# A transformer block on one core: POOL takes more of the quantised feed-forward, ACT's gelu and DVE's next inner row change places with rounding and largest, and the projection's rows are normalised further ahead

## What is computed

```python
x = x + L0_xattn(layernorm(x), ctx)          # 8 heads, 77 keys
x = x + L0_ffn(layernorm(x))                 # below
x = x + L1_xattn(ctx, layernorm(x), mask)    # 4 heads of 64, keys from ctx and x, RMS-normalised
x = x + L1_ffn(layernorm(x))                 # routed experts, top 2 of 8, and a shared one

def bitlinear(x, W, b):                      # per-tensor ternary W, 8-bit rows
    w_scale = clip(mean(|W|), 1e-5); Wq = clip(round(W / w_scale), -1, 1) * w_scale
    x_scale = clip(max(|x|, axis=-1), 1e-5)
    xq = clip(round(x * 127 / x_scale), -128, 127) * x_scale / 127
    return xq @ Wq.T + b
def L0_ffn(x):                               # 256 -> 1024 -> 256
    return bitlinear(gelu(bitlinear(x, W1, b1)), W2, b2)
```

## Time and profile before

| | |
|---|---|
| median of 3 runs | 929.47 us (927.81 to 930.09) |
| the profiled execution | 928.22 us |
| its span, first to last instruction | 926.5 us |
| mean granted clock of PE | 0.987 of full speed |
| feed-forward | about 53 to 142 us of the span |
| projection to the start of attention | about 127 to 200 us |

### The profile page before, as it was taken

How to read it: one execution, slowest core, us unless ns; L and a number is a source line. 1 busy time by engine, 2 the same in 40 slices (tenths; PEclk the granted TensorE clock), 3 DMA queues, 4 the chain that set the end, 5 groups by cost and what they waited for, 6 DMA issues and landing times.

```text
span 926.5 us, 14997 instructions
## 1 busy us (share of the span) xinstructions
PE 866.8 (94%) x4299; PEld 611.3 (66%) x4300; DVE 630.7 (68%) x1275; ACT 532.6 (57%) x851; POOL 388.9 (42%) x334
## 2 busy tenths in 40 slices
PE   9977789889999999999999999999999999999992
PEld 4635455545555555555457887878888888888881
DVE  5788987855567557456488779846666666666666
ACT  2558885445665765775554534326666666666650
POOL 2144455435676746756515545512222222222210
PEclk9999999989999999999999999999999999999997
DMA  9400000009478578569565100078711298526405
GB/s 310 110 1 1 0 1 1 1 5 364 160 292 328 194 305 326 219 269 350 199 262 196 82 1 1 12 316 342 305 40 36 71 348 341 208 88 254 116 9 182
DMA packets 49909, 154.07 MB, mean 166 GB/s; under 512 B 6266, under 2 KB 24438, under 8 KB 44236
## 3 DMA queue, kind: packets, MB, share of 16 engines
q1 hardware_dynamic: 46124, 144.25, 41.4%
q0 software_dynamic: 3744, 9.31, 3.1%
HBM read 97.85 MB, written 56.62 MB: 167 GB/s over the span
## 4 chain that ended last, share of the span: by engine, by line
PE 67%; DVE 17%; ACT 6%; issue 3%; DMA 3%; POOL 2%; SPq 1%; DVEq 0%; ACTq 0%; POOLq 0%
PE banks L1047 11%; PE banks L1300 8%; PE banks L1302 8%; PE banks L1301 8%; PE banks L1015 4%; PE banks L1039 3%; PE banks L1040 3%; DVE small L2105 2%; PE banks L1337 2%; PE banks L1339 2%; PE banks L1338 2%; PE banks L1313 2%; PE banks L953 2%; PE banks L919 1%; PE banks L1061 1%
## 5 line engine op out<-in xcount | busy, mean ns | idle before, releaser
L1047 PE MATMUL banks<-wexp 128*65 128x512 f32 (+1 forms) x288 | 149.9, 602 | 3.5 <-ACT wexp L1614 3.5
L677 POOL TENSOR_TENSOR cv_hl<-wexp,cv_hl 128x1024 fp32r<-128x1024 f32 x45 | 108.6, 2421 | 56.0 <-ACT cv_hl L1591 55.4
L1300 PE MATMUL banks<-ring,x_hi 128*128 x312 | 127.5, 408 | 0.0
L1302 PE MATMUL banks<-ring,x_lo 128*128 x312 | 122.1, 391 | 0.0
L1301 PE MATMUL banks<-ring,x_hi 128*128 x312 | 122.0, 391 | 0.0
L1614 ACT ACTIVATE wexp<-banks 128x512 f32<-128x512 f32 x128 | 76.4, 599 | 64.2 <-PE banks L1040 63.8
L2105 DVE TENSOR_REDUCE small<-banks 128x1 bf16<-128x1107 f32 x64 | 84.1, 1314 | 38.4 <-PE banks L1015 38.4
L1750 ACT ACTIVATE banks<-wexp 128x1024 f32 x72 | 73.5, 1021 | 47.7 <-DVE aux L2496 47.7
L1728 ACT ACTIVATE aux<-banks 128x512 f32<-128x512 f32 x78 | 46.7, 599 | 61.2 <-PE banks L1302 45.2
L1039 PE MATMUL banks<-q_hi,k_hl 128*128 128x512 f32 x144 | 76.7, 533 | 1.9 <-ACT q_lo L1582 1.0
L1302 PEld LDWEIGHTS banks<-ring,x_lo 128*128 128x128 f32 x312 | 58.6, 188 | 13.2
(11 more groups left out here) (374 smaller groups left out, 2171.5 us busy)
## 6 DMA issues: line engine op xcount, KB each, us to landing
wsplit<-cv_hl SPq DMA_DIRECT2D x45, 1024.0 KB, 8.0
ring<-wsplit SPq DMA_DIRECT2D x32, 1280.0 KB
wexp<-in_L_ffn_w SPq DMA_DIRECT2D x40, 512.0 KB, 5.9
wexp<-in_expert_biases SPq DMA_DIRECT2D x8, 1152.0 KB, 6.6
ring<-wsplit SPq DMA_DIRECT2D x4, 1024.0 KB, 8.2
wexp<-moe_y SPq DMA_DIRECT2D x7, 512.0 KB, 6.1
wexp<-in_L_ffn_sw SPq DMA_DIRECT2D x5, 512.0 KB, 9.0
x_sb<-in_x SPq DMA_DIRECT2D x4, 512.0 KB, 7.6
```

Of the source, the lines that this page charges most:

```text
L677: g.tensor_tensor(sides(hl[:, PIECE:2 * PIECE]), raw, sides(hl[:, 0:PIECE]).bitcast(f32), ALU.subtract).then_inc(s['cv_lo'], 1)
L1047: mm(pb[5 + half][0:DA, :], vh[b][0:w, c, :], pT[q % 3][0:w, :], start=c == 0, stop=c == len(KTILES) - 1).then_inc(s['a_pv'], 1)
L1300: mm(o[:], x_hi[u][:, kc, :], hi, start=kc == 0 and not primed, stop=False, skip_group_check=primed)
L1302: last = mm(o[:], x_lo[u][:, kc, :], hi, start=False, stop=primed and kc == KC - 1, skip_group_check=primed)
```

## The change

It moves work between engines and changes the order in two queues.

- DVE's `ffn_sum` is gone. ACT scales the second layer's result out of PSUM into one of two new buffers `y_part`, and POOL adds it to `x_sb` six tiles behind its normalising. DVE's statistics follow one turn later and wait for POOL (`f_res`).
- POOL rounds the tokens in place of ACT, except for the last tile. Its normalising is written as x * rstd + less_mean, where DVE prepares less_mean = -mean * rstd. The constants of attention, which it set after the feed-forward, are set between the tiles.
- ACT's gelu of tile i+2 comes before the rounding of tile i+1.
- DVE's row of tile i+2 comes before the two largest of the turn.
- PE turns tile i+4's tokens in turn i, between the second layer of tile i and the transposes of tile i+1.
- In the projection, tiles 6 and 7 are normalised and the scales of tiles 8 to 15 are made before any squares are summed; after that tile t+6 is normalised in step t, where it was t+4.
- Two semaphores for constants are merged into one, which does not change the order of anything, and the matmuls that fill a pause in turn -3 write another bank.

```diff
@@ POOL
+            def ffn_tokens(t):
+                g.tensor_scalar(xn[:, t % 2, :], xn[:, t % 2, :], f_by[:, t % 2, 0:1], MAGIC, ALU.mult, ALU.add).then_inc(s['f_xm'], 1)
+            def ffn_result(t):
+                pool.wait_ge(s['f_yout'], t + 1)
+                g.tensor_tensor(x_sb[:, t, :], x_sb[:, t, :], y_part[t % 2], ALU.add).then_inc(s['f_res'], 1)
             for t in range(T):
                 if t == TB:
                     pool.wait_ge(s['f_rstd'], 2)
                 if t >= 2:
                     pool.wait_ge(s['f_xqT_full'], t - 1)
-                g.tensor_scalar(xn[:, t % 2, :], x_sb[:, t, :], mv[:, t, 0:1], rstd[:, t:t + 1], ALU.subtract, ALU.mult).then_inc(s['f_xn'], 1)
+                g.tensor_scalar(xn[:, t % 2, :], x_sb[:, t, :], rstd[:, t:t + 1], less_mean[:, t:t + 1], ALU.mult, ALU.add).then_inc(s['f_xn'], 1)
+                if t >= 1:
+                    pool.wait_ge(s['f_by'], t)
+                    ffn_tokens(t - 1)
                 pool.wait_ge(s['f_xn'], t + 1)
-                if t >= 5:
-                    pool.wait_ge(s['f_by'], t)
                 g.tensor_tensor(x_sb[:, t, :], x_sb[:, t, :], b2_all[:], ALU.add).then_inc(s['f_pool'], 1)
+                if t >= 6:
+                    ffn_result(t - 6)
+                if 8 <= t < 13:
+                    pool.wait_ge(s['f_res'], t - 5)
+                    attention_constants(t - 8)
...
+            for t in range(T - 6, T):
+                ffn_result(t)
@@ PE, ffn_turn
                 if there(i + 3):
                     ffn_in(i + 3, 1 - u)
                 if there(i):
                     ffn_out(i, u)
+                if there(i + 4):
+                    ffn_tokens_T(i + 4, u)
                 if there(i + 1):
                     ffn_hidden_T(i + 1, 1 - u)
@@ ACT
-                if there(tokens):
+                if isinstance(tokens, int) and tokens == T - 1:
                     a(xn[:, u, :], xn[:, u, :], ACT.Copy, scale=f_by[:, u, 0:1], bias=MAGIC).then_inc(s['f_xm'], 1)
...
+            def ffn_sum(t, u):
+                act.wait_ge(s['f_y'], t + 1)
+                act.wait_ge(s['f_by'], t + 5)
+                if not isinstance(t, int) or t >= 2:
+                    act.wait_ge(s['f_res'], t - 1)
+                a(y_part[u], pb[6][:, 0:D], ACT.Copy, scale=f_step[:, 1 - u, 1:2]).then_inc(s['f_yout'], 1)
             def ffn_turn(i, u):
-                if there(i + 3):
-                    ffn_T(i + 3, 1 - u)
+                if there(i - 1):
+                    ffn_sum(i - 1, 1 - u)
                 if there(i):
                     ffn_hidden_T(i, u)
+                if there(i + 2):
+                    ffn_act(i + 2, u)
                 if there(i + 4) or there(i + 1):
                     ffn_quantise(i + 4, i + 1, i, u)
-                if there(i + 2):
-                    ffn_act(i + 2, u)
+                if there(i + 4):
+                    ffn_T(i + 4, u)
@@ DVE
             def ffn_scales(t0, t1):
                 norm(t0, t1, 0.0)
-                ve.sem_inc(s['f_rstd'], 1)
+                v.scalar_tensor_tensor(less_mean[:, t0:t1], mv[:, t0:t1, 0], -1.0, rstd[:, t0:t1], ALU.mult, ALU.mult).then_inc(s['f_rstd'], 1)
...
             def ffn_turn(i, u):
-                if there(i - 1):
-                    ffn_sum(i - 1, 1 - u)
                 if there(i + 1):
                     ve.wait_ge(s['f_acc'], i + 2)
...
-                if there(i - 1):
-                    ffn_statistics(i - 1)
+                if there(i + 2):
+                    ffn_hidden(i + 2, u)
                 if there(i + 4):
                     last = ffn_tokens(i + 4, u)
                 if there(i + 1):
                     last = ffn_largest(i + 1, 1 - u)
...
                     ffn_factors(u, c)
-                if there(i + 2):
-                    ffn_hidden(i + 2, u)
+                if there(i - 2):
+                    last = ffn_statistics(i - 2)
@@ DVE, projection
+            for t in range(6, TB):
+                proj_tokens(t)
+            scales(LN_EARLY, T, ln_r, 1.0 + LN_EPS, LN_EPS ** 2)
             for t in range(T):
...
-                if 6 <= t + 4 < T:
-                    proj_tokens(t + 4)
+                if TB <= t + 6 < T:
+                    proj_tokens(t + 6)
                 proj_squares(t)
-                if t == 3:
-                    scales(LN_EARLY, T, ln_r, 1.0 + LN_EPS, LN_EPS ** 2)
```

More of the change, by code:

```diff
@@ L192, in program @@
         h_qT = [scr.take(HID, HC, bf16) for _ in range(2)]
+        y_part = [scr.take(D) for _ in range(2)]
         assert scr.at <= mark
@@ L272, in program @@
         ln_r = sb("ln_r", [P, T])
+        less_mean = sb("less_mean", [P, T])
         gateT = sb("gateT", [P, KC, E])
@@ L784, in full, with warm @@
                 last.then_inc(s['prep_full'], 1)
-            def warm(n):
+            def warm(n, o=pb[7]):
                 for _ in range(n):
-                    mm(pb[7][:], ones_b[:], ones_b[:].unsqueeze(1).to_broadcast([P, 4, P]), start=True, stop=True)
-            pe.wait_ge(s['warm'], 1)
+                    mm(o[:], ones_b[:], ones_b[:].unsqueeze(1).to_broadcast([P, 4, P]), start=True, stop=True)
+            pe.wait_ge(s['const'], 2)
             warm(28)
-            pe.wait_ge(s['const'], 2)
+            pe.wait_ge(s['const'], 3)
             pe.wait_ge(s['ld_l0'], NLD['ld_l0'])
@@ L898, in _, with ffn_tokens_T @@
             pe.wait_ge(s['f_pre'], 2)
-            def ffn_in(t, u):
+            def ffn_tokens_T(t, u):
                 pe.wait_ge(s['f_xm'], t + 1)
@@ L904, in ffn_in @@
                 last.then_inc(s['f_xqT_full'], 1)
+            def ffn_in(t, u):
                 pe.wait_ge(s['f_xqT'], t + 1)
@@ L964, in between @@
                 if i == -3:
-                    warm(WARM_FFN)
+                    warm(WARM_FFN, pb[5])
                 if i == T - 4:
@@ L1983, in ffn_hidden @@
                 v.scalar_tensor_tensor(h_f[u], banks[:, 2 * (1 - u) * 512:2 * (2 - u) * 512], f_step[:, u, 0:1], b1_all[:], ALU.mult, ALU.add).then_inc(s['f_acc'], 1)
-            def ffn_sum(t, u):
-                ve.wait_ge(s['f_y'], t + 1)
-                ve.wait_ge(s['f_pool'], t + 1)
-                v.scalar_tensor_tensor(tile(t), pb[6][:, 0:D], f_step[:, 1 - u, 1:2], tile(t), ALU.mult, ALU.add)\
-                    .then_inc(s['f_yout'], 1)
             def ffn_statistics(t):
-                ve.wait_ge(s['f_yout'], t + 1)
-                statistics(t)
+                ve.wait_ge(s['f_res'], t + 1)
+                return statistics(t)
             def ffn_turn(i, u):
-                if there(i - 1):
-                    ffn_sum(i - 1, 1 - u)
                 if there(i + 1):
@@ L2002, in ffn_turn @@
                     c = slice(0 if there(i + 3) else 1, 2 if there(i) else 1)
+                    if not isinstance(i, int) or i >= 2:
+                        ve.wait_ge(s['f_yout'], i - 1)
                     last = v.tensor_tensor(f_step[:, 1 - u, c], f_max[1 - u][:, c], wsc[:, c], ALU.mult)
-                    if not there(i + 1):
+                    if isinstance(i, int) and i < 0:
                         link(last)
-                if there(i - 1):
-                    ffn_statistics(i - 1)
+                    elif not there(i + 1):
+                        last.then_inc(s['f_by'], 1)
+                        ve.wait_ge(s['f_by'], i + 5)
+                if there(i + 2):
+                    ffn_hidden(i + 2, u)
                 if there(i + 4):
@@ L2015, in ffn_turn @@
                     ffn_factors(u, c)
-                if there(i + 2):
-                    ffn_hidden(i + 2, u)
+                if there(i - 2):
+                    last = ffn_statistics(i - 2)
+                    if isinstance(i, int) and i == T - 7:
+                        link(last)
             ss_l = p0[:].rearrange("p a b -> p (a b)")
```

23 lines of the change are left out of this document (16 added, 7 removed).

## The result

The change makes the kernel slower: a median of 958.95 us against 929.06 (927.81 to 930.09) on the same chip, ratio 1.0315 (1.0291 to 1.0339). One of its four executions was slow (1183.65 us) and is left out of the ratio; the other three took 955.89 to 959.03 us (median 958.88). That is +29.9 us where +24.1 was forecast, and inside the range. The profiled execution took 959.03 us.

The account below looks back on a forecast made before the run. PE, busy for 94% of the span, was taken as the kernel's bound, DVE as the feed-forward's. To the end of tile 13's transposes 22.7, then 1.0, projection 0.4: +24.1 us on 929.47, say 953.5, range 944.5 to 961.

Parts of the forecast that it names:

- The loop through the two buffers: Feed-forward: DVE's early row waits for transposes that free its buffer, closing a one-turn loop of 5.56 us, before 4.40.
- POOL's rounding at 1.22 us, a turn of 6.0: Feed-forward: POOL's token rounding takes 1.22 us and delays PE's eight transposes, adding 0.45 to a turn: 6.0 us.
- The clock, a rival with 0.20: Feed-forward loop: PE's clock falls in half the turns, transposes take about 0.7 us more, 4.6 in all: 958; chance 0.20.
- quick rounding: Rival, feed-forward: POOL rounds quickly, 12 x 0.45 less in the turns and 0.4 on the way in: 948; chance 0.23.
- The way in, +0.7: Up to row 2 of the feed-forward: POOL's rounding, less_mean and a later gelu table cost +0.7 us (0 to 1.5).
- The end of the feed-forward: Tile 13's transposes end at 150.2 us, +22.7; on to projection tile 3, gelu before tile 14's rounding adds +1.0.
- ACT's order, no price of its own in the turn: Feed-forward: with gelu ahead of rounding and the other swaps, ACT's turn stays near 3.7 us.
- The projection, +0.4: From projection tile 3 on: later squares on POOL against some savings, net +0.4 us, between -2 and +3.3.
- a sign that the prediction had set for itself as one of being wrong: Projection: the distance from tile 3 to head 0's transposes changing by over 3 us would make the prediction wrong.
- my upper bound of 3.3: Projection: POOL's backlog of squares arrives in full at head 0's transposes, +3.3 us.
- The 2 us that I took off for engines standing ready: Projection: ACT will stand ready, with no projection rows queued ahead of the root, so 2 us of the backlog is hidden.
- the 0.9 at the end: Projection: three normalisings gone from DVE's queue behind the mean squares give some 0.9 us back.

Follow-up runs that it names:

- before_multiply_add: The kernel before, with POOL's normalising written as a multiplication and an addition in place of a subtraction and a multiplication: 925.17 us, ratio 0.9953.
- fill_pe: The kernel after, with eight matmuls of 256 columns, whose result nothing reads, added in PE's pause in each turn: 952.11 us, ratio 1.0265.
- dve_order_back: The kernel after, with DVE's row of tile i+2 alone back at the end of its turn: 939.98 us, ratio 1.0125.
- proj_order_alone: The kernel before, with only the projection's order of the kernel after: 926.03 us, ratio 0.9968.
- pool_split_new_loop: The kernel after, with POOL squaring projection tiles 0 and 1 between its last results and DVE summing those squares before the scales: 955.29 us, ratio 1.0292.
- before_row_first: The kernel before, with DVE writing the row of tile i+2 ahead of the two largest: 951.95 us, ratio 1.025.
- dve_act_order_back: The kernel after, with DVE's row and ACT's gelu back in their old places: 929.23 us, ratio 1.0002.

## Why the prediction was right, and where it was not

*The loop through the two buffers.* Shown in both directions: the order alone makes it in the kernel before (+23 us), the order undone or a third buffer takes it away. It was right step by step and not only in its sum: in the turn shown no step is more than 0.06 us from the working. Its warm length, 5.50 to 5.58, is the 5.56 of the working.

*POOL's rounding at 1.22 us, a turn of 6.0.* Wrong: 0.47, and the turn of 5.56 held. The term was mis-sized because L616, the nearest row, owes its length to its form (subtract and multiply), which `before_multiply_add` shows. Twelve turns at 6.0 gave 72.0 us; they took 68.94.

*The clock, a rival with 0.20.* That the clock falls is in the earlier trace rows; the 0.7 us that a cold turn was to take more, and the half of the turns that were to be cold, were estimates that no run shows: it was 0.47 to 0.90, in three turns of twelve. The fall came beside quick rounding, though with shorter turns than I had joined it to. The cold turns cost 0.90 + 0.47 + 0.57 = 1.9 us over 5.55 from row 2 to 14; row 1 to row 2 is 6.42 (0.9; granted clock 0.50 from 73.59 to 75.11); tile 13's transposes 1.86 (0.8; 0.54 while they run); tile 0 of the projection 4.36 for 2.75 (1.6; 0.50 from 152 to 154). That is 5.2 up to projection tile 3; `fill_pe`, warm in all of them, is 4.6 shorter from row 0 (61.79) to tile 3 (160.75) than after. I had 4.6 for this rival. Rounding that was quicker than forecast (12 x 0.45 = 5.4 less) and a colder clock (5.2 more) about cancel. Two terms were wrong by some 5 us each, in opposite directions, so the closeness of the total is luck.

*The way in, +0.7.* Wrong, +2.8. Row 2 is the first to need a used buffer, so row 1 to row 2 is already a turn of the loop: 4.19 before, 5.58 in `fill_pe` (68.01 to 73.59), 6.42 cold. I counted the loop from row 2 on and should have counted 13 turns.

*The end of the feed-forward.* 22.7 and +1.0 forecast, 22.5 and 2.0 measured. That 22.5 meets 22.7 is luck: quick rounding took 5.4 off, the cold clock put 3.6 on up to there, and the thirteenth turn, which I had not counted, 1.4 (5.58 for 4.19). The excess of the second is the cold tile 0.

*ACT's order, no price of its own in the turn.* The turn shown bears that out, since the longer loop hides it. It is not free in general: with DVE's row back in its place it costs some 10 us (`dve_order_back`).

*The projection, +0.4.* The step that failed most: +5.0 to the first score. From tile 3 to head 0's transposes it is 28.44 us for 25.21, 3.2 more, and over 3 was a sign that the prediction had set for itself as one of being wrong; so was a granted clock other than the 1.00 that it forecast for the feed-forward (0.92 from row 2 to row 14). The reason given held: squares of tile 2 at 9.5 us after tile 3 (forecast 9), mean squares at 20.5 (21), head 0's transposes 3.2 later, my upper bound of 3.3. In the 9.5 some luck is hidden: the scales started at 3.7 for 3, their chain took 4.7 for 6, and the last 1.1, mostly DVE's sum of tile 0's squares, was not in my 9. The 2 us that I took off for engines standing ready and the 0.9 at the end were not there. From mean squares to head 0's transposes it is 7.96 us, before 7.48.

But against `proj_order_alone` (6.3 from tile 3 to the squares of tile 2) it is not the order that costs. After has 3.1 us more there: 1.1 because tile 15's statistics wait for the result's new way through ACT and POOL (tile 3 + 1.8 for + 0.7), 0.7 for two rows normalised beside POOL's squares (1.46 for 0.73), and 1.3 for the chain of scales beside them. Another 0.9 lies between mean squares and head 0 (7.96 for 7.08, of which L2101 itself is 0.8, held beside POOL), and 2.3 behind it, where PE is cold behind a pause of 4.71 us (1.97 and 4.25 us for 1.09 and 2.75; granted clock 0.50 from 194.65 to 196.62). With the order's own gain, -1.4, this makes 4.9 of the 5.0. So the loss belongs to the part that I had down as a gain without a price, POOL's larger share: its results stand in front of its squares, and some of DVE's small instructions (L1905, L2101) end only with its own. The split of POOL's queue gives some 3 us of medians back, within touching intervals.

*The sum.* In medians +29.9 for +24.1: of the 6.7 that the span is over the sum, the turns are -3.0, the way in 2.1, the two stretches behind the loop 1.7, the projection and what follows 5.9.

Open is why three turns of twelve go cold when PE's pauses in front of all are alike (before L924 1.57, 1.57 and 1.71 us in the cold turns, up to 1.72 in warm ones). In `pool_split_new_loop`, the same loop, it is other turns: those that end at 87.04, 104.58 and 122.11 (6.27, 6.45 and 6.45 us), where in after they end at 92.64, 115.25 and 132.51. Open too is what PE's own new order is worth: its queue is the third that the change reorders, and no run undoes that. In the turn shown it costs nothing, as the two token transposes are through (102.35) before ACT's rounding ends (102.47).

## What to carry to other kernels

With two buffers, an instruction that refills one may stand no earlier in its queue than the work that frees the other: lay out the way from refill to release, and count every engine's queue on it, and every turn from the first reuse. A part that frees the busiest engine is worth its work only if what it queues on the other engine is in front of nothing that is due; here the work moved to POOL, with the orders back, gained up to 4 us in the loop and lost them at the next stage, until two pieces were taken out of the line. Where a loop leaves PE pauses like those here (1.57 and 1.71 us in front of the cold turns of after, 2.20 in the turn shown of `before_row_first`), look at the granted clock before costing its transposes, and behind the loop too (4.71 us in front of head 0).

## What the runs showed of the hardware

- POOL's tensor_scalar on 128 x 256 takes 1224 ns as subtract and multiply with two scalars from memory, 555 as multiply and add with two (`before_multiply_add`), and 475 as multiply and add with one scalar and a constant (L614, after).
- Some of DVE's instructions, small as they are, ended when POOL's did: L1905 on 8 columns 1.03 us (170.53 to 171.56) beside POOL's L676 (170.49 to 171.53), the mean squares L2101 1.00 beside one from 186.61 to 187.65. Where POOL was idle the first took 0.17 (`proj_order_alone`, 145.54); the second took 0.20 before. Not every instruction took longer: a sum of squares (L2060) took 0.67, usually 0.64, beside L672 in `dve_act_order_back` (149.84), and the statistics L1887 the usual 0.43 beside L672 in after (168.02). So POOL's time had a price here where DVE runs a chain of small steps on the critical path: the chain of scales took 4.73 us beside POOL's squares and 3.41 where POOL was idle.
- PE's granted clock fell in three turns of twelve (0.50 from 90.60 to 91.60, from 114.20 to 115.20 and from 131.50 to 133.00), while PE was busy for 46.3 of the 69 us from row 2 to row 14, two thirds; with eight more matmuls a turn (`fill_pe`) it was 1.00 from 77 to 175 us, and 0.50 from 74 to 76, ahead of the first of them (76.53). A slice of 2 us with 0.43 us of work stood in front of one fall (88 us) and in front of none at 100 us.
